# Three PSUM banks for the scores and one for the value products in a global attention loop

## The chip, the cores and the metric

The kernel runs on one NeuronCore of a Trainium2 chip. The metric is the device time of one execution in microseconds (us), as the median of several runs. Four engines compute: PE (TensorE, matrix products; PEld is its weight load), DVE (VectorE), ACT (ScalarE) and POOL (GpSimd). SP (SyncE) issues the transfers. Each engine works through its own queue in order, and the queues are tied together by semaphores alone. PSUM, where PE writes, has eight banks of 512 fp32 columns in each of 128 partitions.

## What is computed

The reference is a transformer block on a batch of 4 sequences of 1024 tokens and 128 channels. A modulated layer norm is followed by global attention with 16 heads of width 8, then by another modulated layer norm and six layers of local attention and a gated feed-forward net. The change is in global attention only:

```
scores = einsum('bhqd,bhkd->bhqk', q, k) / sqrt(8)
attn = softmax(scores, axis=-1)
out = einsum('bhqk,bhkd->bhqd', attn, v)
```

## The kernel before

The function `global_attention` covers 4 batches times 16 heads as `NG` = 16 groups of `GH` = 4 heads. Each group has two halves (`qh`) of 512 queries, and each half has 8 steps, one for each block of 128 keys (`kb`); a group so has 16 steps `s`. A half group is 8 steps. Three kinds of work are interleaved, and the order of each engine is written out by hand.

- **Scores.** `score(g, s, c)` is one matmul of 128 keys by 512 queries for head `c` (line 566), into a bank of `p_s`. ACT takes its exponential into `E` (line 706), in fp32. `p_s` has two banks, so score n waits until exponential n-2 is done.
- **Value products.** `weigh(g, s, halves)` multiplies `E` of the step before with the values, for four heads side by side in four column groups (line 583), and accumulates over the 8 steps into one bank of `p_o` for each `qh`. It is cut into two halves of 256 queries, except for the first key block of a half group, which is done in one piece of 512. It waits for all four exponentials of its step. The value rows carry a one, so that the sum of the exponentials comes out as a further column.
- **Maxima for later work.** The softmax needs the row maxima before the exponentials. A *unit* is two matmuls of 128 queries by 512 keys (line 546) into one of two slots of `p_max`, two banks each, and a DVE reduction over its 1024 columns (line 640). Unit k waits until reduction k-2 is done. A half group needs 16 units. They are computed 11 steps and less ahead, two in each step (`units(g, s)`): the first beside scores 0 and 1, the second beside scores 2 and 3. The rows of the operands are laid out so that a unit and the scores beside it lie in different row halves of the array (rows 0 to 49, and rows 64 to 113), and run together as a pair.

Twice in a group, at `s % 8 == 5`, the 16 unit maxima of a half group are turned by a PE transpose (`max_rows`, line 555), split by DVE into two bf16 parts (lines 649 and 651) and written by four SP transfers (line 491) as two further rows of `QA`. The scores of that half group, from step `s % 8 == 0` on, wait for them on `s_md`. The transpose reads what the last reduction wrote, and it lies in the ring of `p_max` slots. In these steps ("late" in the code) both units of the step come after the transpose, so that scores 0 and 1 have no unit beside them, the first unit is issued with scores 2 and 3 of its own row half, and the second alone.

Twice in a group the value products are finished: ACT copies `p_o` to `OE` (line 697) after the exponentials of step `s % 8 == 2`, PE transposes `OE` back into the same bank of `p_o` at the end of step `s % 8 == 3` (line 591, four transposes), and DVE takes the reciprocal and multiplies into `AO` (lines 658 and 661).

PSUM is full: 4 banks for `p_max`, 2 for `p_s`, 2 for `p_o`. The order on PE in an ordinary step is S0 M1a, S1 M1b, W0, S2 M2a, S3 M2b, W1. Here S is a score, M a matmul of a unit, and W half of a value product, which is of the step before.

Of the kernel before, what the change touches and what calls it, by code (L numbers as in the profile page):

```python
# [9 lines left out]
ALU = mybir.AluOpType  # L10
# [3 lines left out]
P = 128  # L14
# [24 lines left out]
NG = B * HG  # L39
# [381 lines left out]
def global_attention(nc, ins, w):  # L421
# [18 lines left out]
    s_mx = m.count("s_mx", 2 * HU + 2)  # L440
    s_mr = m.count("s_mr", 2 * HU + 2)
    s_mb = m.count("s_mb", 2)
# [4 lines left out]
    s_oe = m.count("s_oe", 2)  # L447
    s_ot = m.count("s_ot", 2)
    s_rc = m.count("s_rc", 2)
    s_ao = m.count("s_ao", 2)  # L450

# [21 lines left out]

    def begun_with(g):

        return [(0, 0, i) for i in range(HU)], [(0, 1, i) for i in range(6)]

    def on_sp(sp):
# [7 lines left out]
        def max_rows(g, qh):  # L486
            sp.wait_ge(s_mr.sem, s_mr.at(g, (qh + 1) * (HU + 1)))
# [46 lines left out]
    def on_pe(pe):  # L534
        pe.wait_ge(s_z.sem, 3)

        def max_unit(g, qh, i, parts=(0, 1)):
            k = qh * (HU + 1) + i
            c, qt = unit(i)
            o, cb = place(c)  # L540
            if 0 in parts and g * (2 * HU + 2) + k >= 2:
                pe.wait_ge(s_mr.sem, g * (2 * HU + 2) + k - 1)
            if 0 in parts and i == 0 and qh == 0:
                pe.wait_ge(s_ld[g % 3].sem, s_ld[g % 3].at(g // 3))
            for j in parts:
                mm = pe.matmul(p_max[:, k % 2, j * 512:(j + 1) * 512],  # L546
                               QA[o:o + MROW, g % 3, qh, cb, qt * P:(qt + 1) * P],
                               KA[o:o + MROW, g % 3, cb, j * 512:(j + 1) * 512], start=True, stop=True)
            if 1 in parts:
                mm.then_inc(s_mx.sem, 1)  # L550

        def max_rows(g, qh):
            k = qh * (HU + 1) + HU
            pe.wait_ge(s_mr.sem, s_mr.at(g, k))
            pe.transpose(p_max[0:GH * 4, k % 2, 0:P], negmax[:, qh, :, :].rearrange("p c q -> p (c q)"),
                         ident[:, :]).then_inc(s_mx.sem, 1)

        def score(g, s, c):
            qh, kb = divmod(s, 8)
            i = 4 * s + c  # L560
            if 64 * g + i >= 2:
                pe.wait_ge(s_ex.sem, 64 * g + i - 1)
            if kb == 0 and c == 0:
                pe.wait_ge(s_md.sem, s_md.at(g, 64 * (qh + 1)))
            o, cb = place(c)
            pe.matmul(p_s[:, i % 2, :], KA[o:o + KROWS, g % 3, cb, kb * P:(kb + 1) * P],  # L566
                      QA[o:o + KROWS, g % 3, qh, cb, :], start=True, stop=True).then_inc(s_st.sem, 1)

        def weigh(g, s, halves):
            qh, kb = divmod(s, 8)  # L570
            if kb == 0:
                if 0 not in halves:
                    return
                lo, hi = 0, 512
            else:
                lo, hi = 256 * halves[0], 256 * (halves[-1] + 1)
            pe.wait_ge(s_ex.sem, s_ex.at(g, 4 * s + 4))
            if s == 0:
# [6 lines left out]
            if hi == 512:  # L585
                mm.then_inc(s_pv.sem, 1)

        def result(g, qh):
            pe.wait_ge(s_oe.sem, s_oe.at(g, qh + 1))
# [4 lines left out]
        before, after = begun_with(0)  # L594
        for u in before:
            max_unit(*u)
        max_rows(0, 0)
        for u in after:
            max_unit(*u)
        for g in range(NG):  # L600
            for s in range(16):
                todo = units(g, s)
                late = s % 8 == 5
                w_ = (g, s - 1) if s > 0 else (g - 1, 15) if g > 0 else None
# [4 lines left out]
                if todo and not late:  # L609
                    max_unit(*todo[0], (1,))  # L610
                if w_:
                    weigh(*w_, (0,))
                if s == 5:
                    max_rows(g, 1)
                if s == 13 and g + 1 < NG:
                    max_rows(g + 1, 0)
                score(g, s, 2)
                if todo:
                    max_unit(*todo[0 if late else 1], (0,))
                score(g, s, 3)  # L620
                if todo:
                    max_unit(*todo[0 if late else 1], (1,))
                if w_:
# [7 lines left out]
        weigh(NG - 1, 15, (0, 1))  # L631
        result(NG - 1, 1)

    def on_dve(dve):

        def max_unit(g, qh, i):
            k = qh * (HU + 1) + i
            c, qt = unit(i)
            dve.wait_ge(s_mx.sem, s_mx.at(g, k + 1))
            dve.tensor_reduce(negmax[:, qh, c, qt:qt + 1], p_max[:, k % 2, :], axis=AX.X, op=ALU.max,  # L640
                              negate=True).then_inc(s_mr.sem, 1)

        def max_rows(g, qh):
            k = qh * (HU + 1) + HU
            dve.wait_ge(s_mx.sem, s_mx.at(g, k + 1))
            if g > 0:
# [7 lines left out]
        def result(g, qh):  # L654
            b, hg = divmod(g, HG)
            dve.wait_ge(s_ot.sem, s_ot.at(g, qh + 1))
            o = p_o[:, qh, :].rearrange("p (q c w) -> p q c w", q=4, w=VW)
            dve.reciprocal(rsum[:, qh, :, :], o[:, :, :, DH]).then_inc(s_rc.sem, 1)
# [3 lines left out]
                              in1=rsum[:, qh, :, :].unsqueeze(3).broadcast_to([P, 4, GH, DH]),  # L662
                              op=ALU.mult).then_inc(s_ao.sem, 1)

        before, after = begun_with(0)
        for u in before:
            max_unit(*u)
        max_rows(0, 0)
        for u in after:
            max_unit(*u)  # L670
        for g in range(NG):
            for s in range(16):
                todo = units(g, s)
                late = s % 8 == 5
                if todo and not late:
                    max_unit(*todo[0])
                if s == 5:
                    max_rows(g, 1)
                if s == 13 and g + 1 < NG:
                    max_rows(g + 1, 0)  # L680
                if todo:
                    max_unit(*todo[0 if late else 1])
                if todo and late:
                    max_unit(*todo[1])
                if s == 3 and g > 0:
                    result(g - 1, 1)
                if s == 11:
                    result(g, 0)
        result(NG - 1, 1)

    def on_act(act):

        def result_copy(g, qh):
            act.wait_ge(s_pv.sem, s_pv.at(g, 8 * (qh + 1)))
            if g > 0:
                act.wait_ge(s_ot.sem, s_ot.at(g - 1, qh + 1))
            act.activation(OE[:, qh, :], p_o[:, qh, :], ACT.Copy).then_inc(s_oe.sem, 1)

        for g in range(NG):
            for s in range(16):  # L700
                for c in range(GH):
                    i = 4 * s + c
                    act.wait_ge(s_st.sem, s_st.at(g, i + 1))
                    if c == 0 and 16 * g + s >= 4:
                        act.wait_ge(s_pv.sem, 16 * g + s - 3)
                    act.activation(E[:, s % 4, c, :], p_s[:, i % 2, :], ACT.Exp, scale=DH ** -0.5)\  # L706
# [1054 lines left out]
```

## Time and profile before

| what | us |
|---|---|
| median of 3 runs | 3910.28 |
| lowest and highest run | 3904.84, 3911.35 |
| span of the profiled execution, first to last instruction | 3903.5 |
| first to last exponential of global attention (line 706) in it | 138.6 to 841.3 |

The profile shows one execution. The span is its time from its first instruction to its last; the page gives no time around it, so that the distance to the median of the runs, 6.8 us, stands for what lies around it and for the spread. Global attention is the stretch from about 111 to 845 us. Before it lie the modulation and the projections, behind it the residual and the six layers, some 3050 us that the change does not touch.

### The profile page before, as it was taken

To read this page: it belongs to the slowest core of one execution; us is meant where nothing else is said; L and a number is where in the kernel's file an instruction comes from. 1 tells how busy PE (TensorE), PEld (TensorE's weight loads), DVE (VectorE), ACT (ScalarE), POOL (GpSimd) and SP (SyncE) were. 2 spreads that over 40 slices of the span, in tenths; PEclk is the share of its full clock that TensorE was granted. 3 is DMA by queue.
4 is the path that set the end of the run, shared out by engine and by line. 5 is a ranking of instruction groups with operands and counts; after the bars stand their busy time and mean duration, and the time that the engine had idled before them with its cause. 6 is when DMAs were issued, how large, how long until landed. Compare 5 with 4: busy or idle time off the path is not lost. (4 is left out here: it accounts for less than half of the span.)

```text
span 3903.5 us, 161387 instructions
## 1 busy us (share of the span) xinstructions
PE 3703.2 (95%) x70608; PEld 2688.4 (69%) x70608; DVE 3274.0 (84%) x4767; ACT 2854.2 (73%) x5060; POOL 2384.1 (61%) x1968
## 2 busy tenths in 40 slices
PE   5899999976999999999999999999999999999997
PEld 3222222235888888888888888888888888888885
DVE  7899899956888888888888888888888888888884
ACT  2488888865777777777777777777777777777774
POOL 2000000017777777877778777777777777777784
PEclk7799999998999999999999999999999999999999
DMA  2110000003444344344443344443443443443442
GB/s 89 34 50 26 18 21 18 14 17 107 113 106 116 103 118 119 103 111 111 111 120 108 104 118 111 113 115 104 110 119 108 116 109 103 130 113 103 115 109 56
DMA packets 202559, 360.11 MB, mean 92 GB/s; under 512 B 35518, under 2 KB 74050, under 8 KB 201538
## 3 DMA queue, kind: packets, MB, share of 16 engines
q1 hardware_dynamic: 201794, 348.71, 33.1%
q8 instruction: 627, 10.27, 1.1%
q14 instruction: 138, 1.13, 0.1%
HBM read 236.68 MB, written 111.67 MB: 89 GB/s over the span
## 5 line engine op out<-in xcount | busy, mean ns | idle before, releaser
L1121 POOL TENSOR_TENSOR T<-T 128x1024 f32<-128x1024 f32 x384 | 908.1, 2377 | 27.0 <-DVE T L1600 26.1
L1139 POOL TENSOR_TENSOR T<-T,rn 128x1024 f32<-128x1024 f32 x384 | 731.4, 1905 | 27.1 <-POOL rn L1132 0.4
L706 ACT ACTIVATE E<-p_s 128x512 f32<-128x512 f32 x1024 | 555.8, 596 | 169.4 <-PE p_s L566 164.2
L640 DVE TENSOR_REDUCE negmax<-p_max 128x1 f32<-128x1024 f32 x512 | 605.7, 1221 | 52.1 <-PE p_max L546 38.6
L1211 PE MATMUL PA<-Wqkv,XS 128*128 128x512 f32 x2304 | 633.3, 410 | 10.0 <-DVE XS L1561 8.1
L1211 PEld LDWEIGHTS PA<-Wqkv,XS 128*128 128x128 f32 x2304 | 415.4, 194 | 80.3 <-DVE XS L1561 10.1
L1608 DVE TENSOR_REDUCE ss<-SQ 128x32 f32<-128x2048 f32 x192 | 436.8, 2275 | 0.0
L1239 PE MATMUL PD<-ident,T 128*128 128x128 f32 x3072 | 409.3, 276 | 6.6 <-POOL T L1139 6.4
L1287 PEld LDWEIGHTS PB<-ET,VW 64*64 64x64 f32 x24576 | 377.1, 135 | 53.9 <-DVE T L1600 29.6
L1287 PE MATMUL PB<-ET,VW 64*64 64x32 f32 x24576 | 399.0, 220 | 15.9 <-DVE T L1600 9.6
L1300 PEld LDWEIGHTS PD<-Wo,OT 128*128 128x128 f32 x3072 | 366.2, 192 | 62.1 <-issue 62.1
L1427 ACT ACTIVATE SQ<-PA 128x1024 f32<-128x1024 f32 x192 | 196.9, 1025 | 271.9 <-PE PA L1211 271.9
L1579 DVE TENSOR_REDUCE sm<-Ew 128x16 f32<-128x1024 f32 x192 | 233.6, 1217 | 190.6 <-ACT Ew L1441 190.6
L566 PE MATMUL p_s<-QA,KA 50*128 50x512 bf16 x1024 | 360.6, 387 | 29.4 <-ACT E L706 14.8
L1300 PE MATMUL PD<-Wo,OT 128*128 128x128 f32 x3072 | 378.6, 277 | 5.1 <-ACT OT L1455 3.1
L546 PE MATMUL p_max<-KA,QA 48*128 48x512 bf16 x1024 | 361.5, 397 | 12.9 <-PEq L417 8.8
L1115 POOL TENSOR_TENSOR Ew<-Ew,sm 128x1024 f32<-128x1024 f32 x192 | 365.7, 1905 | 12.3 <-DVE sm L1584 12.3
L1595 DVE TENSOR_TENSOR T<-PA,tab 128x1024 f32<-128x1024 f32 x192 | 234.4, 1221 | 157.9 <-ACT SQ L1427 157.9
L1239 PEld LDWEIGHTS PD<-ident,T 128*128 128x128 f32 x3072 | 337.9, 141 | 26.8 <-ACT qT L1470 6.0
L1211 PE MATMUL PB<-Wqkv,XS 128*128 128x512 f32 x1152 | 337.4, 428 | 0.0
L583 PE MATMUL p_o<-E,VG 128*32 128x512 f32 (+1 forms) x3832 | 321.9, 408 | 0.1
L1261 PE MATMUL PC<-kT,qT 64*32 64x64 f32 x24576 | 294.1, 224 | 22.3 <-issue 22.3
(168 smaller groups left out, 6809.6 us busy)
## 6 DMA issues: line engine op xcount, KB each, us to landing
VW<-v_rows SPq DMA_DIRECT2D x768, 256.0 KB, 4.4
v_rows<-Vs SPq DMA_DIRECT2D x192, 512.0 KB, 6.0
Wraw<-in_Wqkv SPq DMA_DIRECT2D x40, 192.0 KB, 5.1
QA<-parts_q SPq DMA_DIRECT2D x384, 16.0 KB
KA<-parts_k SPq DMA_DIRECT2D x192, 32.0 KB
parts_q<-parts SPq DMA_DIRECT2D x8, 384.0 KB, 2.6
parts_k<-parts SPq DMA_DIRECT2D x8, 384.0 KB, 2.6
Wo<-in_Wo SPq DMA_DIRECT2D x12, 256.0 KB, 4.8
```

The source lines that it names most:

```text
L546: mm = pe.matmul(p_max[:, k % 2, j * 512:(j + 1) * 512], QA[o:o + MROW, g % 3, qh, cb, qt * P:(qt + 1) * P], KA[o:o + MROW, g % 3, cb, j * ...
L566: pe.matmul(p_s[:, i % 2, :], KA[o:o + KROWS, g % 3, cb, kb * P:(kb + 1) * P], QA[o:o + KROWS, g % 3, qh, cb, :], start=True, stop=True).t ...
L640: dve.tensor_reduce(negmax[:, qh, c, qt:qt + 1], p_max[:, k % 2, :], axis=AX.X, op=ALU.max, negate=True).then_inc(s_mr.sem, 1)
L706: act.activation(E[:, s % 4, c, :], p_s[:, i % 2, :], ACT.Exp, scale=DH ** -0.5)\
L1115: pool.tensor_tensor(out=e, in0=e, in1=sm[:, p, 1, :].unsqueeze(2).broadcast_to([P, LH, KW]), op=ALU.mult).then_inc(pn.sem, 1)
L1121: pool.tensor_tensor(out=t_, in0=t_, in1=T2[:, i * HALF:(i + 1) * HALF], op=ALU.add).then_inc(ad.sem, 1)
L1139: pool.tensor_tensor(out=t_, in0=t_, in1=rn[:, p, i * LH:(i + 1) * LH].unsqueeze(2).broadcast_to([P, LH, LD]), op=ALU.mult).then_inc(no.se ...
L1211: mm = pe.matmul(pair[:, half, :], XS[:, b, i, 1:P + 1], Wqkv[:, l % 2, j, lo:lo + 512], start=(k == 0), stop=(k == 2))
L1239: mm = pe.transpose(flat(PD)[:, j * P:(j + 1) * P], T1[:, n % 2, lo:lo + P], ident[:, :])
L1287: mm = pe.matmul(PB[c * LD:(c + 1) * LD, par, i * P + q:i * P + q + WIN], VW[o:o + KW, p, v, j * LD:(j + 1) * LD], ET[o:o + KW, j, q:q + WIN],
L1300: mm = pe.matmul(PD[:, 0, 0:D], OT[:, j, :], Wo[:, l % 2, j, :], start=(j == 0), stop=(j == PAIRS - 1))
L1608: dve.reduce_sum(ss[:, p, :], heads(SQ[:, :]), axis=AX.X).then_inc(ssq.sem, 1)
```

## The change

`p_s` gets a third bank and `p_o` gives one up. From this follow the other edits:

- Score n takes bank n mod 3 and waits for exponential n-3.
- Both halves `qh` accumulate into the one bank of `p_o`. The first value product of a half group waits until ACT has copied the result of the half group before (`s_oe`). The copy moves from behind the exponentials of step 2 (mod 8) to behind those of step 0. The first key block is cut into two halves like the others.
- The transposed result no longer goes back into `p_o` but takes a slot in the ring of the maxima (`turn`, `turns`). `s_ot` and `s_ao` go; `s_mx` and `s_mr` count all turns of the ring.
- The order in steps 3 and 5 (mod 8) changes: the transposes of the result, or of the maxima, come behind the first half W0 of the value product, between the first and the second unit of the step, on PE as on DVE. The late step goes: its first unit stands beside scores 0 and 1 again and its second beside scores 2 and 3.
- In step 1 (mod 8) score 2 and the first matmul of the second unit come ahead of W0.

```diff
-    p_s = m.ps("p_s", [P, 2, 512])
-    p_o = m.ps("p_o", [P, 2, 512])
+    p_s = m.ps("p_s", [P, 3, 512])
+    p_o = m.ps("p_o", [P, 512])
...
+    ROWS, RESULT = HU, HU + 1
+
+    def extra(g, s):
+
+        if s == 5:
+            return [(g, 1, ROWS)]
+        if s == 13 and g + 1 < NG:
+            return [(g + 1, 0, ROWS)]
+        if s == 3 and g > 0:
+            return [(g - 1, 1, RESULT)]
+        if s == 11:
+            return [(g, 0, RESULT)]
+        return []
+
+    before = [(0, 0, i) for i in range(HU)] + [(0, 0, ROWS)] + [(0, 1, i) for i in range(6)]
+    turns = list(before)
+    for g in range(NG):
+        for s in range(16):
+            turns += units(g, s)[:1] + extra(g, s) + units(g, s)[1:]
+    turns.append((NG - 1, 1, RESULT))
+    turn = {item: k for k, item in enumerate(turns)}
...
+        def free(k):
+            if k >= 2:
+                pe.wait_ge(s_mr.sem, s_mr.at(k - 2))
...
         def score(g, s, c):
             qh, kb = divmod(s, 8)
-            i = 4 * s + c
-            if 64 * g + i >= 2:
-                pe.wait_ge(s_ex.sem, 64 * g + i - 1)
+            n = 64 * g + 4 * s + c
+            if n >= 3:
+                pe.wait_ge(s_ex.sem, n - 2)
...
-            if kb == 0 and g > 0:
-                pe.wait_ge(s_ao.sem, s_ao.at(g - 1, qh + 1))
+            if kb == 0 and half == 0 and g + qh > 0:
+                pe.wait_ge(s_oe.sem, s_oe.at(g, qh))
             for c in range(GH):
-                mm = pe.matmul(p_o[c * VW:(c + 1) * VW, qh, lo:hi], VG[:, g % 2, kb, c, :], E[:, s % 4, c, lo:hi],
-                               start=(kb == 0), stop=(kb == 7), skip_group_check=True)
+                mm = pe.matmul(p_o[c * VW:(c + 1) * VW, lo:hi], VG[:, g % 2, kb, c, :], E[:, s % 4, c, lo:hi],
+                               start=(kb == 0 and half == 0), stop=(kb == 7), skip_group_check=True)
...
         def result(g, qh):
+            k = turn[g, qh, RESULT]
+            free(k)
             pe.wait_ge(s_oe.sem, s_oe.at(g, qh + 1))
             for qt in range(4):
-                mm = pe.transpose(p_o[:, qh, qt * P:(qt + 1) * P], OE[:, qh, qt * P:(qt + 1) * P], ident[:, :])
-            mm.then_inc(s_ot.sem, 1)
+                mm = pe.transpose(p_max[:, k % 2, qt * P:(qt + 1) * P], OE[:, qh, qt * P:(qt + 1) * P], ident[:, :])
+            mm.then_inc(s_mx.sem, 1)
...
                 score(g, s, 0)
-                if todo and not late:
-                    max_unit(*todo[0], (0,))
+                if one:
+                    max_unit(one, (0,))
                 score(g, s, 1)
...
+                if s % 8 == 1:
+                    score(g, s, 2)
+                    if two:
+                        max_unit(two, (0,))
+                if done:
+                    weigh(*done, 0)
+                for item in extra(g, s):
+                    turned(item)
+                if s % 8 != 1:
+                    score(g, s, 2)
+                    if two:
+                        max_unit(two, (0,))
                 score(g, s, 3)
-                if todo:
-                    max_unit(*todo[0 if late else 1], (1,))
-                if w_:
-                    weigh(*w_, (1,))
-                if todo and late:
-                    max_unit(*todo[1])
-                if s == 3 and g > 0:
-                    result(g - 1, 1)
-                if s == 11:
-                    result(g, 0)
+                if two:
+                    max_unit(two, (1,))
+                if done:
+                    weigh(*done, 1)
...
-                if s == 2 and g > 0:
+                if s == 0 and g > 0:
                     result_copy(g - 1, 1)
-                if s == 10:
+                if s == 8:
                     result_copy(g, 0)
```

## Rows read from the trace of the kernel before

**Rows 1.** Busy time by stretch: length; PE, PEld, DVE, ACT, POOL; granted clock, DMA share, GB/s.
```profile
230.00:670.00 440.00, 421.49 (x3787) 120.10 (x3788) 398.67 (x402) 357.61 (x664) 11.46 (x13) 1.00 0.09 24
```

**Rows 2.** Line 658, once per half group: 230:670, then all; first, last start.
```profile
L658 DVE RECIPROCAL rsum<-p_o x20: 247/248/248, 239.5 to 657.2; 128x16 f32<-128x16 f32 x20
L658 DVE RECIPROCAL rsum<-p_o x32: 247/248/258, 173.5 to 844.4; 128x16 f32<-128x16 f32 x32
```

**Rows 3.** Waits in 230:670: engine, line, releaser: total us, times, longest.
```profile
PEld p_s L566 <- ACT E L706: 178.2, 400, 1.0
```

**Rows 4.** PE in time order (start, length, instruction, count): scores 0 and 1 of a step.
```profile
533.52 0.39 PE L566 MATMUL p_s<-QA,KA 50*128 50x512 bf16 x1
...
533.95 0.39 PE L566 MATMUL p_s<-QA,KA 50*128 50x512 bf16 x1
```

**Rows 5.** PE in time order: half a step in which no score waits.
```profile
520.65 0.39 PE L566 MATMUL p_s<-QA,KA 50*128 50x512 bf16 x1
...
520.88 0.38 PE L566 MATMUL p_s<-QA,KA 50*128 50x512 bf16 x1
...
521.19 0.64 PE L583 MATMUL p_o<-E,VG 128*32 128x256 f32 x8
521.76 0.39 PE L566 MATMUL p_s<-QA,KA 50*128 50x512 bf16 x1
```

**Rows 6.** Last matmul of a unit, its reduction; two scores, their exponentials.
```profile
519.76 0.39 PE L546 MATMUL p_max<-KA,QA 48*128 48x512 bf16 x1
520.22 1.23 DVE L640 TENSOR_REDUCE negmax<-p_max 128x1 f32<-128x1024 f32 x1
527.62 0.60 PE L566 MATMUL p_s<-QA,KA 50*128 50x512 bf16 x2
528.04 1.08 ACT L706 ACTIVATE E<-p_s 128x512 f32<-128x512 f32 x2 [0.26 <-PE p_s L566]
```

**Rows 7.** PE near the end, no units left: scores that begin two successive steps.
```profile
818.30 0.81 PE L566 MATMUL p_s<-QA,KA 50*128 50x512 bf16 x2
...
820.75 0.81 PE L566 MATMUL p_s<-QA,KA 50*128 50x512 bf16 x2
```

**Rows 8.** PE in time order: transposed result, next score; transposed maxima.
```profile
524.57 0.66 PE L591 MATMUL p_o<-ident,OE 128*128 128x128 f32 x4
525.16 0.39 PE L566 MATMUL p_s<-QA,KA 50*128 50x512 bf16 x1
...
528.72 0.28 PE L555 MATMUL p_max<-ident,negmax 128*16 128x128 f32 x1
```

**Rows 9.** DVE in time order, with the idle time before and its releaser.
```profile
525.28 0.25 DVE L658 RECIPROCAL rsum<-p_o 128x16 f32<-128x16 f32 x1
...
525.84 2.57 DVE L640 TENSOR_REDUCE negmax<-p_max 128x1 f32<-128x1024 f32 x2
529.03 0.28 DVE L649 CAST nmb<-p_max 16x128 bf16<-16x128 f32 x1 [0.62 <-PE p_max L555]
529.35 0.28 DVE L651 TENSOR_TENSOR nmb<-p_max,nmb 16x128 bf16<-16x128 f32 x1
530.00 6.88 DVE L640 TENSOR_REDUCE negmax<-p_max 128x1 f32<-128x1024 f32 x6 [0.38 <-PE p_max L546]
```

**Rows 10.** The last value products (512 wide) and the copy behind them.
```profile
841.91 0.16 PEld L583 LDWEIGHTS p_o<-E,VG 128*32 128x32 f32 x8 [0.63 <-ACT E L706]
843.05 0.60 ACT L697 ACTIVATE OE<-p_o 128x512 f32<-128x512 f32 x1 [1.19 <-PE p_o L583]
```

**Rows 11.** Busy time by stretch; the last two columns are DMA share and GB/s.
```profile
534.00:535.00 1.00, 1.00 (x12) 0.30 (x12) 1.00 (x2) 1.00 (x2) 0.00 (x0) 1.00 0.00 0
```

**Rows 12.** Near the start: a stretch (granted clock 0.50), and PE in it.
```profile
145.70:149.00 3.30, 3.30 (x24) 0.67 (x24) 2.42 (x3) 1.86 (x4) 0.00 (x0) 0.50 0.00 0
146.78 0.60 PE L566 MATMUL p_s<-QA,KA 50*128 50x512 bf16 x1
...
148.76 0.59 PE L566 MATMUL p_s<-QA,KA 50*128 50x512 bf16 x1
```

More of the change, by code:

```diff
@@ L535, in on_pe, with max_unit @@
         pe.wait_ge(s_z.sem, 3)
-        def max_unit(g, qh, i, parts=(0, 1)):
-            k = qh * (HU + 1) + i
+        def free(k):
+            if k >= 2:
+                pe.wait_ge(s_mr.sem, s_mr.at(k - 2))
+        def max_unit(item, parts=(0, 1)):
+            g, qh, i = item
+            k = turn[item]
             c, qt = unit(i)
             o, cb = place(c)
-            if 0 in parts and g * (2 * HU + 2) + k >= 2:
-                pe.wait_ge(s_mr.sem, g * (2 * HU + 2) + k - 1)
+            if 0 in parts:
+                free(k)
             if 0 in parts and i == 0 and qh == 0:
@@ L552, in max_rows @@
         def max_rows(g, qh):
-            k = qh * (HU + 1) + HU
-            pe.wait_ge(s_mr.sem, s_mr.at(g, k))
+            k = turn[g, qh, ROWS]
+            free(k)
+            pe.wait_ge(s_mr.sem, s_mr.at(turn[g, qh, HU - 1]))
             pe.transpose(p_max[0:GH * 4, k % 2, 0:P], negmax[:, qh, :, :].rearrange("p c q -> p (c q)"),
@@ L565, in score, with weigh @@
             o, cb = place(c)
-            pe.matmul(p_s[:, i % 2, :], KA[o:o + KROWS, g % 3, cb, kb * P:(kb + 1) * P],
+            pe.matmul(p_s[:, n % 3, :], KA[o:o + KROWS, g % 3, cb, kb * P:(kb + 1) * P],
                       QA[o:o + KROWS, g % 3, qh, cb, :], start=True, stop=True).then_inc(s_st.sem, 1)
-        def weigh(g, s, halves):
+        def weigh(g, s, half):
             qh, kb = divmod(s, 8)
[L571 to L576, printed above, removed]
+            lo, hi = 256 * half, 256 * (half + 1)
@@ L592, in result, with turned @@
-            mm.then_inc(s_ot.sem, 1)
[L594 to L599, printed above, removed]
+                mm = pe.transpose(p_max[:, k % 2, qt * P:(qt + 1) * P], OE[:, qh, qt * P:(qt + 1) * P], ident[:, :])
+            mm.then_inc(s_mx.sem, 1)
+        def turned(item):
+            g, qh, i = item
+            if i == ROWS:
+                max_rows(g, qh)
+            elif i == RESULT:
+                result(g, qh)
+            else:
+                max_unit(item)
@@ L600, in on_pe @@
+        for item in before:
+            turned(item)
         for g in range(NG):
             for s in range(16):
-                todo = units(g, s)
-                late = s % 8 == 5
-                w_ = (g, s - 1) if s > 0 else (g - 1, 15) if g > 0 else None
+                one, two = units(g, s) or (None, None)
+                done = (g, s - 1) if s > 0 else (g - 1, 15) if g > 0 else None
                 score(g, s, 0)
-                if todo and not late:
-                    max_unit(*todo[0], (0,))
+                if one:
+                    max_unit(one, (0,))
@@ new lines, in on_pe @@
+                if done:
+                    weigh(*done, 0)
+                for item in extra(g, s):
+                    turned(item)
+                if s % 8 != 1:
+                    score(g, s, 2)
+                    if two:
+                        max_unit(two, (0,))
+                score(g, s, 3)
+                if two:
+                    max_unit(two, (1,))
+                if done:
+                    weigh(*done, 1)
+        for half in range(2):
+            weigh(NG - 1, 15, half)
@@ L662, in result, with turned @@
                               in1=rsum[:, qh, :, :].unsqueeze(3).broadcast_to([P, 4, GH, DH]),
[L663 to L670, printed above, removed]
+                              op=ALU.mult).then_inc(s_mr.sem, 1)
+        def turned(item):
+            g, qh, i = item
+            if i == ROWS:
+                max_rows(g, qh)
+            elif i == RESULT:
+                result(g, qh)
+            else:
+                max_unit(item)
+        for item in before:
+            turned(item)
         for g in range(NG):
             for s in range(16):
[L673 to L688, printed above, removed]
+                for item in units(g, s)[:1] + extra(g, s) + units(g, s)[1:]:
+                    turned(item)
         result(NG - 1, 1)
@@ L695, in result_copy @@
             if g > 0:
-                act.wait_ge(s_ot.sem, s_ot.at(g - 1, qh + 1))
-            act.activation(OE[:, qh, :], p_o[:, qh, :], ACT.Copy).then_inc(s_oe.sem, 1)
+                act.wait_ge(s_mx.sem, s_mx.at(turn[g - 1, qh, RESULT]))
+            act.activation(OE[:, qh, :], p_o[:, :], ACT.Copy).then_inc(s_oe.sem, 1)
         for g in range(NG):
```

47 lines of the change are left out of this document (18 added, 29 removed).

## The prediction

> **What bounds the kernel now.** I read the busy time by stretch first. Between 230 and 670 us no engine is full: DVE is busy 398.67 of 440 us (91%), ACT 357.61 (81%), and the clock is granted in full [rows 1]. PE's 96% there is no evidence, since pipelined matmuls look longer than they are. Next comes the period. The reciprocal runs once per half group, and 20 of them span 417.7 us, so that a half group takes 417.7 / 19 = 21.98 us [rows 2]. Third, the waits: the largest of PE is that of a score for an exponential, 178.2 us in 400 pieces [rows 3].
>
> Last, one step in time order. Scores 0 and 1 start 0.43 us apart where one waits [rows 4] and 0.23 us where none does [rows 5]. Score n needs the bank of exponential n-2, and ACT takes 0.49 us from one exponential to the next (1.08 less 0.59) and starts 0.42 us behind its score [rows 6]. A half step without a wait is 0.23 to the second score, 0.31 to the value product and 0.57 to the next score, 1.11 us together [rows 5], and a step 2.22. A step really takes 2.45, also near the end, where no unit and no reduction is left [rows 7]. So it is not DVE that sets the ordinary step, but two score banks: 0.23 us a step.
>
> The rest of 21.98 is 21.98 - 8 x 2.45 = 2.38 us. It lies in the transposed result (0.59 us of PE [rows 8]), the transposed maxima, and the late step, where units and scores don't run as pairs. There DVE stands idle 0.62 us ahead of the maxima and 0.38 behind them [rows 9].
>
> **Part 1, the third bank.** Score n then waits for exponential n-3. In a free half step score 2 comes 1.11 us after score 0 and score 3 at 1.34. The exponential of score 0 starts at 0.42, lasts 0.59, and frees its bank at 1.06 (0.04 for the signal, as between lines 649 and 651: 0.32 less 0.28 [rows 9]). Both are free, and PE alone could do a step in 2.22.
>
> **Part 2, the late step.** Its unpaired matmuls go, two slots of PE of 0.23 for each of two units, some 0.9 us per half group. The transposed maxima hide behind the reduction of the unit ahead of them.
>
> **What is late next: DVE.** Six reductions run back to back in 6.88 us, (6.88 - 1.22) / 5 = 1.13 each [rows 9]. Sixteen take 18.12 us. The reciprocal and product take 0.56 (525.28 to 525.84), the two parts of the maxima 0.32 + 0.28. That is 19.28 us per half group, while PE needs 8 x 2.22 + 0.59 + 0.28 = 18.6. PE runs only 0.04 us a step ahead of DVE, so DVE paces.
>
> **The ring's bubbles.** A reduction starts 0.46 us after its last matmul [rows 6], and the slot is free 1.22 + 0.04 = 1.26 after its own start. Let R be the start of a reduction.
> - Ordinary: unit k starts at R(k-2) + 1.26, its reduction could start at + 0.23 + 0.46, so at 1.95. DVE is free at 2 x 1.13 = 2.26. No bubble, 0.31 spare.
> - Result (step 3): the turn between the units takes a slot. The second unit waits for the first reduction: 1.26 + 0.69 = 1.95 after it. DVE would be free at 1.13 + 0.56 = 1.69. Bubble 0.26. The transposes start one value product behind the first pair, and reach DVE 0.71 later (524.57 to 525.28), at 1.13 after the first reduction's start: just in time.
> - Maxima (step 5): likewise, 1.95 against 1.13 + 0.60 = 1.73. Bubble 0.22.
> - Step 1: W0 stands between the two matmuls of the second unit: 1.26 + 0.31 + 0.57 + 0.46 = 2.60 against 2.26. Bubble 0.34.
>
> So a half group takes 19.28 + 0.82 = 20.1 us, 1.88 less than now. The trace has no result in the ring. Bounds: 19.3, if the bubbles vanish, and 20.8, if scores still wait (second rival).
>
> **Part 3, one bank for value products.** The last half product of a half group (W1 of step 0 of the next) is followed by the copy, and the copy by W0 of step 1. The eight records of a half product end 0.64 us after its start [rows 5]. With a signal (0.04), the copy (0.60) and a signal W0 may start 1.32 us after W1 began. An upper bound is the product of 512 queries, which reached its copy 1.14 us after its start [rows 10]: 1.78. In between PE has 0.57 of W1, then 0.23 + 0.23 for three pairs, and 0.31: 1.34. On PE alone that just covers it. Where the ring holds the second unit back (the bubble of step 1), W0 comes 0.34 us later and there is 0.36 to spare. I take nothing; the upper bound would cost 0.1 a half group. If the cover were gone, each us of delay would cost one per half group, with score 3 and its unit queued behind on PE, and DVE waiting for that unit. The copy also moves ahead of the exponentials of step 1 on ACT, which slip by some 0.3 us; the third bank takes that up. The first key block in two parts takes two half steps like all others: nothing.
>
> **Part 4, the maxima's rows.** SP's four transfers follow line 651, whose start is 529.35, and by 534.0 no DMA moves anything [rows 11]: under 4.65 us. Now line 651 starts 1.13 + 0.32 = 1.45 after the first reduction of step 5, and score 0 of step 8 comes 1.95 + 5 x 1.13 = 7.6 less 0.69, less up to 0.2 of lead, = 6.7 after it. That leaves 5.3 us: covered, by 0.6 at least. SP's head loads are issued at other times, and are not moved past anything.
>
> **The sum.** From the first reciprocal, at 173.5, on, 29 intervals are of the ordinary kind [rows 2]: 29 x 1.88 = 55. Before it lie 11 steps, from the first exponential at 138.6 on. The first of them run at half clock, where a half step takes 1.98 us [rows 12] and an exponential is done in time: nothing. The 8 or so behind them save a half group's worth, 2. In the last group, steps 5 to 15 have no unit and PE paces; those and the step behind save 0.23 each [rows 5, 7], 12 x 0.23 = 2.8, less 0.1 for the last product in two parts. Together 60 us. The span of 3903.5 becomes 3844. The median of the runs lies 6.8 above the span, so 3910.3 - 60 = **3850 us**.
>
> **A rule weighed.** DVE is the busiest engine that can be judged, at 91% [rows 1]. The Trainium skill (Perfetto Trace Analysis, "Identifying the Most-Contended Engine") wants the engine with the highest occupancy optimized first. By that rule two score banks would matter little. The row speaks against it, since a step is as long without DVE's work [rows 7]. By the rule part 1 brings nothing and the time is that of the second rival below, 3875; by the row it is 3850.
>
> **Rivals.**
> - *The bubbles vanish.* The lead of PE is enough, and DVE runs through at 19.3. For it: six back to back reductions. Against: in steps 1, 3 and 5 the slot, not PE, is late. 29 x 0.82 = 24 more, 3826 us. Chance 0.08.
> - *The third bank's gain doesn't arrive.* The value product waits for all four exponentials; in a free step the last of them ends less than 0.1 us before W0 is due, so that a slightly longer chain would hold PE in place of the score. Steps stay at 2.45; the late step's part and the rest remain: 8 x 2.45 + 0.59 + 0.28 + 0.34 = 20.8, saving 1.17 x 29 + 1 = 35, 3875 us. Against: DVE's pace loosens it by 0.04 a step. Chance 0.15.
> - *No gain at all*, since the single bank or the rows of the maxima eat it: 3903 to 3915. Chance 0.03.
> - *Slower: the single bank is a chain.* If the copy came 0.36 + 1.88 = 2.2 us later than worked out, W0 of step 1 would hold PE, then DVE, for longer than all that is saved; each further us costs 31 us. Against: only a copy that starts behind the exponentials of step 1 would be so late (four take some 2.5 us), and the order on ACT excludes that. At 3.2 us later: 3941. Chance 0.03.
> - *Slower: the clock falls.* At 0.50 a half step took 1.98 us [rows 12] against 1.11. If more than 15% of the stretch ran so, the gain would be gone; at 30% some 3945 us. Against: the grant is 1.00 over 440 us though PE waits 400 times for a bank [rows 1, 3], and the change takes waits away. Chance 0.02. The Trainium skill (TensorE: Matmul & The Clock Gate, "A second HAM failure mode: psum-queue depth-cycling") tells of a kernel whose cycling through banks made the grant swing between both levels; this trace, which cycles two rings of banks, doesn't agree.
>
> **How the numbers follow.** Forecast 3850, its own band 3840 to 3862, chance 0.69. The range must hold 0.8: 3834 to 3876 takes in the second rival, but leaves out most of the first. A run of this kernel tells 0.2%, 8 us, from no change; faster has 0.69 + 0.08 + 0.15 = 0.92, same 0.03, slower 0.05.
>
> **What would show it.** Reciprocals 20.1 us apart. Waits of line 566 for ACT nearly gone, those of line 546 for DVE up. DVE near 96% busy, with a gap of 0.2 to 0.35 us in steps 1, 3 and 5. No idle time of PE ahead of W0 in step 1. It would be wrong if ordinary steps stayed at 2.45, if the period were above 20.8, or if the layers behind the stage moved.

## The result and the profile after

The changed kernel takes 3849.6 us (median of 4 runs, 3847.4 to 3853.6) against 3910.8 for the kernel before (median of 4 runs, 3904.8 to 3917.0). The ratio is 0.984, with a 95% interval of 0.982 to 0.985: 1.6% faster. Measured again in later rounds it was 0.984 (0.982 to 0.986).

| what, us | before | after |
|---|---|---|
| median | 3910.8 | 3849.6 |
| span of the profiled execution | 3903.5 | 3851.6 |
| one half group | 21.98 | 20.06 |
| first exponential (138.6, 137.9) to last reciprocal (844.4, 781.6) | 705.8 | 643.7 |

The stage gives back 62 us. The two spans differ by only 52. The remaining 10 lie behind the stage, in layers whose code is the same; other runs of the changed kernel had spans of 3845 to 3848, so I take this for the spread of single executions; the medians are 61 us apart. The profiled run of the changed kernel took 3853.6 us as timed from outside and 3851.6 by its span, so that 2 us lie around a span and not 6.8. The rest of the 6.8 was spread.

Busy time by stretch of the changed kernel, columns as in [rows 1]:

```profile
230.00:670.00 440.00, 430.68 (x4322) 114.31 (x4314) 423.78 (x440) 391.87 (x728) 12.36 (x15) 1.00 0.10 26
```

And its reciprocal, for 230 to 670 us and in all, as in [rows 2]:

```profile
L681 DVE RECIPROCAL rsum<-p_max x22: 246/248/249, 248.1 to 669.6; 128x16 f32<-128x16 f32 x22
L681 DVE RECIPROCAL rsum<-p_max x32: 246/248/258, 167.9 to 781.6; 128x16 f32<-128x16 f32 x32
```

DVE has gone from 398.67 to 423.78 of 440 us, 96%. Most reciprocals are 20.06 apart; in three intervals between 248 and 349 us it is 20.12, so that the 22 here give 421.5 / 21 = 20.07. In each of those three (at 254.5, 294.7 and 334.9 us) ACT has one more copy to make, of a weight for the layers behind (line 728). The order of DVE, to be held against [rows 9]:

```profile
501.94 2.35 DVE L662 TENSOR_REDUCE negmax<-p_max 128x1 f32<-128x1024 f32 x2
504.56 4.62 DVE L662 TENSOR_REDUCE negmax<-p_max 128x1 f32<-128x1024 f32 x4 [0.27 <-PE p_max L567]
509.10 0.25 DVE L681 RECIPROCAL rsum<-p_max 128x16 f32<-128x16 f32 x1
509.38 0.29 DVE L684 TENSOR_TENSOR AO<-p_max,rsum 128x128 f32<-128x128 f32 x1
509.87 4.63 DVE L662 TENSOR_REDUCE negmax<-p_max 128x1 f32<-128x1024 f32 x4 [0.20 <-PE p_max L567]
514.42 0.27 DVE L671 CAST nmb<-p_max 16x128 bf16<-16x128 f32 x1
514.72 0.28 DVE L673 TENSOR_TENSOR nmb<-p_max,nmb 16x128 bf16<-16x128 f32 x1
515.20 9.15 DVE L662 TENSOR_REDUCE negmax<-p_max 128x1 f32<-128x1024 f32 x8 [0.20 <-PE p_max L567]
```

One half group is all in these rows. DVE stands idle three times, 0.27 us in step 1, 0.20 behind the result in step 3, 0.20 behind the maxima in step 5, and the rows show no other idle time. The 0.62 and 0.38 around the maxima [rows 9] are gone. PE in time order, the second half of step 0 and the first of step 1:

```profile
521.19 0.39 PE L588 MATMUL p_s<-QA,KA 50*128 50x512 bf16 x1
...
521.42 0.38 PE L588 MATMUL p_s<-QA,KA 50*128 50x512 bf16 x1
...
521.73 0.64 PE L600 MATMUL p_o<-E,VG 128*32 128x256 f32 x8
522.30 0.39 PE L588 MATMUL p_s<-QA,KA 50*128 50x512 bf16 x1
...
522.75 0.39 PE L588 MATMUL p_s<-QA,KA 50*128 50x512 bf16 x1
523.27 0.39 PE L567 MATMUL p_max<-KA,QA 48*128 48x512 bf16 x1
523.59 0.64 PE L600 MATMUL p_o<-E,VG 128*32 128x256 f32 x8
```

Scores 2 and 3 of step 0 start 0.23 us apart: no score waits. In step 1 (from 522.30) score 2 goes at once, and the unit beside it 0.52 us later, when its slot is free. W0 follows at the usual distance, 0.32, so the copy does not hold it.

One view misleads. The waits of line 588, the score, for ACT have not "nearly gone":

```profile
PEld p_s L588 <- ACT E L720: 136.9, 351, 0.4
PEld p_max L567 <- DVE negmax L662: 27.6, 66, 0.6
```

There are 351 of them, of 0.4 us at most, where [rows 3] had 400, up to 1.0. This is the idle time of the *weight load*. Its loads for a value product take 0.16 us, the product 0.57, and the next score's load comes 0.41 after them whether anything holds it or not; the view puts the gap to the semaphore that the load checks. Of the 178.2 us of [rows 3] most was this too, by an estimate: 0.41 us behind each of some 300 value products make 123. The waits of the unit's load for DVE did go up, as forecast, from 9.8 us in 20 pieces to 27.6 in 66. What told the bank's price was the distance between two score matmuls, 0.43 against 0.23 [rows 4, 5].

### The profile page after: what moved, and what is told of

Read it like the earlier page. It is cut to its first block and busy times, and to the rows that moved or that the text cites. A ratio compares the mean times of both kernels' runs of the same rounds, so it can differ in the third digit from the quotient of the medians.

```text
span 3851.6 us, 161980 instructions
## 1 busy us (share of the span) xinstructions
PE 3659.9 (95%) x70872; PEld 2666.8 (69%) x70872; DVE 3254.8 (85%) x4767; ACT 2855.0 (74%) x5060; POOL 2384.5 (62%) x1968
## 3 DMA queue, kind: packets, MB, share of 16 engines
q14 instruction: 138, 1.13, 0.1%
## 5 line engine op out<-in xcount | busy, mean ns | idle before, releaser
L662 DVE TENSOR_REDUCE negmax<-p_max 128x1 f32<-128x1024 f32 x512 | 589.5, 1218 | 29.3 <-PE p_max L567 29.3
L567 PE MATMUL p_max<-KA,QA 48*128 48x512 bf16 x1024 | 324.2, 394 | 25.6 <-DVE negmax L662 12.4
L600 PE MATMUL p_o<-E,VG 128*32 128x256 f32 x4096 | 327.9, 392 | 0.6 <-ACT E L720 0.4
L588 PE MATMUL p_s<-QA,KA 50*128 50x512 bf16 x1024 | 320.6, 385 | 0.0
```

The costliest lines, as they stand in the source:

```text
L567: mm = pe.matmul(p_max[:, k % 2, j * 512:(j + 1) * 512], QA[o:o + MROW, g % 3, qh, cb, qt * P:(qt + 1) * P], KA[o:o + MROW, g % 3, cb, j * ...
L600: mm = pe.matmul(p_o[c * VW:(c + 1) * VW, lo:hi], VG[:, g % 2, kb, c, :], E[:, s % 4, c, lo:hi], start=(kb == 0 and half == 0), stop=(kb = ...
```

## The experiments

Theory: (a) before, the two score banks set the pace of ordinary steps, not DVE; (b) in the changed kernel DVE sets it, plus a bubble (a gap on DVE that comes back in every half group) at each of three places of the ring of slots; (c) the single bank for value products costs nothing as long as its copy is covered. Rivals: DVE paced both kernels and the gain is the late step's; PE or the exponentials pace both; the bubbles are late transposes. The time of a half group is the distance that nearly all neighbouring reciprocals of a trace have.

**The third bank taken away again.**

```diff
-    p_s = m.ps("p_s", [P, 3, 512])
+    p_s = m.ps("p_s", [P, 2, 512])
...
-            if n >= 3:
-                pe.wait_ge(s_ex.sem, n - 2)
+            if n >= 2:
+                pe.wait_ge(s_ex.sem, n - 1)
```

> The changed kernel with all its new orders, but with two score banks: score n waits for exponential n-2 again. My theory (two score banks hold PE 0.23 us in each ordinary step, and DVE's pace is not what set the kernel before): seven steps of 2.45, and step 1, where score 2 now has to wait for the exponential behind the copy, of some 3.1, with 0.59 + 0.21 for the transposes: 20.8 to 21.0 us per half group against 20.06, so 22 to 27 us slower than the changed kernel, 3872 to 3877. Rival (DVE alone paces and the third bank is idle, all the gain is the late step's): 20.06 and 3850, within 4 us.

Measured: 3896.6 us, ratio to the kernel before 0.997 (0.995 to 0.998); a half group takes 21.49. The third bank is worth 1.43 us a half group in this order, and the rival that gave it nothing falls. My number, 20.8 to 21.0, was too low by 0.5 or more. PE in step 1 (mod 8):

```profile
506.87 0.38 PE L588 MATMUL p_s<-QA,KA 50*128 50x512 bf16 x1
...
507.92 0.39 PE L588 MATMUL p_s<-QA,KA 50*128 50x512 bf16 x1 [0.67 <-ACT E L720]
...
509.70 0.39 PE L588 MATMUL p_s<-QA,KA 50*128 50x512 bf16 x1
```

Score 2 waits for the exponential that now stands behind the copy, as expected; the step takes 3.06. The miss is in steps 3 and 5. I had added the transposes' time on PE (0.59 and 0.21), but the unit behind them waits for its slot, and both steps take 3.08, 0.63 more than an ordinary one. 3.06 + 2 x 3.08 + 5 x 2.45 = 21.5. Step 1 holds 0.61 more than an ordinary step, and 0.24 more than step 1 of the kernel before, which takes 2.82: by the row, score 2 waits 0.67, and in that kernel it doesn't wait there. The new order of step 1 and place of the copy cost this where there are two banks.

**The late step put back.** Three score banks, but steps 3 and 5 in the order of the kernel before; the order of the ring's turns, and of DVE, follows.

```diff
+                late = s % 8 == 5
+                beside = one if late else two
                 score(g, s, 0)
-                if one:
+                if one and not late:
                     max_unit(one, (0,))
...
+                if late and two:
+                    max_unit(two)
+                if not late:
+                    for item in extra(g, s):
+                        turned(item)
```

> The changed kernel with three score banks, but with the order of the kernel before in steps 3 and 5 (mod 8): the result's transposes at the end of the step, the maxima's ahead of both units. My theory: the maxima's turn has nothing to hide behind, so that DVE stands idle some 0.45 us ahead of it and 0.43 behind it in place of 0.20 in all, while the result's bubble stays about 0.25: some 20.7 us per half group against 20.06, 15 to 22 us slower than the changed kernel, 3865 to 3872. Rival (the late step's cost is taken up by the three banks, PE has lead enough): within 4 us of 3850.

Measured: 3875.6 us, 0.991 (0.989 to 0.993); a half group takes 20.95, 0.89 more than in the changed kernel. DVE around the maxima:

```profile
509.04 0.28 DVE L685 CAST nmb<-p_max 16x128 bf16<-16x128 f32 x1 [0.62 <-PE p_max L583]
509.35 0.28 DVE L687 TENSOR_TENSOR nmb<-p_max,nmb 16x128 bf16<-16x128 f32 x1
510.01 10.27 DVE L676 TENSOR_REDUCE negmax<-p_max 128x1 f32<-128x1024 f32 x9 [0.38 <-PE p_max L573]
```

The 0.62 and 0.38 of [rows 9] are back to the digit. I had worked out 0.45 and 0.43; the first is longer because PE has the value product to issue between the last reduction and the transpose. So the order of steps 3 and 5, the late step above all, is worth 0.9 of the 1.92, and what is left for the third bank and the rest is 1.0. The two prices, 1.43 and 0.89, add up to more than 1.92, since each was taken with the rest of the change in place, and with two banks that rest has the wait of 0.67 in step 1. No run shows the third bank without the other edits; its bank comes from `p_o`.

**Half a reduction, in both kernels.** Each maximum is taken over the first 512 keys; the softmax is then shifted by another number. The edit is the same in both:

```diff
-            dve.tensor_reduce(negmax[:, qh, c, qt:qt + 1], p_max[:, k % 2, :], axis=AX.X, op=ALU.max,
+            dve.tensor_reduce(negmax[:, qh, c, qt:qt + 1], p_max[:, k % 2, 0:512], axis=AX.X, op=ALU.max,
```

> The kernel before with each maximum taken over 512 of the 1024 keys. My theory (in the kernel before the two score banks pace the ordinary step): ordinary steps stay at 2.45; only PE's waits for a reduction in the late step can go, 0.41 ahead of the maxima's transpose and 0.49 behind it: 21.98 falls to between 21.1 and 21.98, 0 to 28 us faster than the kernel before, 3882 to 3911. Rival (DVE, the busiest engine, paced it): the half group falls to 19 or less, 85 us or more faster, below 3830.

> The changed kernel with each maximum taken over 512 of the 1024 keys, so that a reduction takes about half the time; the softmax is shifted by another number, which changes rounding alone or lets exponentials grow. My theory (DVE paces the changed kernel): the pace passes to PE, 8 x 2.21 + 0.59 + 0.21 = 18.5, plus 0.2 of waiting for the copy in step 1: 18.7 us per half group against 20.06, some 40 us faster than the changed kernel, 3805 to 3813. Rival (the chain of scores and exponentials, or PE, still paces): 20.06, 3845 to 3853.

Measured on the kernel before: 3888.2 us, 0.995 (0.993 to 0.997); a half group 21.60, 0.38 less. With 0.5 us less work in each of 16 reductions, little moves. The 0.38 does not come from the late step, where I had looked for it (step 5 still takes 3.3), but from steps 1 and 6, which fall from 2.82 to 2.61 and from 2.61 to 2.45. DVE's share falls from 91% to 56% (245.74 of 440), the ordinary step stays at 2.45, and a score still waits in it; here it is score 3:

```profile
510.58 0.39 PE L566 MATMUL p_s<-QA,KA 50*128 50x512 bf16 x1
...
511.03 0.39 PE L566 MATMUL p_s<-QA,KA 50*128 50x512 bf16 x1
```

Measured on the changed kernel: 3807.9 us, 0.974 (0.972 to 0.976); a half group 18.89, 1.17 less. Now DVE waits in each half step, and PE paces at 1.11:

```profile
513.42 0.69 DVE L662 TENSOR_REDUCE negmax<-p_max 128x1 f32<-128x512 f32 x1 [0.41 <-PE p_max L567]
514.53 0.69 DVE L662 TENSOR_REDUCE negmax<-p_max 128x1 f32<-128x512 f32 x1 [0.41 <-PE p_max L567]
```

The same edit is worth 0.38 us in the one and 1.17 in the other. That is (a) and (b) in one pair: the change moved the pace of the ordinary step from the score banks to DVE. At 18.9 it is PE that paces, with 0.2 of waiting for the copy in it.

**Step 1 in the ordinary order.** W0 ahead of score 2.

```diff
-                if s % 8 == 1:
-                    score(g, s, 2)
-                    if two:
-                        max_unit(two, (0,))
                 if done:
                     weigh(*done, 0)
...
-                if s % 8 != 1:
-                    score(g, s, 2)
-                    if two:
-                        max_unit(two, (0,))
+                score(g, s, 2)
+                if two:
+                    max_unit(two, (0,))
```

> The changed kernel, with the order of step 1 (mod 8) as in all other steps: W0 ahead of score 2 and of the second unit. My theory: the bubble of step 1 (0.34 worked out) goes, and a wait of W0 for the copy comes in its place. By the changed kernel's trace the copy ends 1.52 us after W1 began and W0 would be due at 1.11: 0.41 of waiting, of which DVE's lead leaves 0.24. Half group 19.9 to 20.0 against 20.06, some 3 us faster than the changed kernel, 3846. Rival (the order of step 1 is needed to cover the copy on the one bank for value products): half group 20.4 or more, 10 us or more slower.

Measured: 3848.2 us, 0.983 (0.980 to 0.986); a half group 20.02. The trace shows the trade: W0 now waits for the copy, and DVE's gap of step 1 is 0.24 in place of 0.27.

```profile
506.02 4.62 DVE L657 TENSOR_REDUCE negmax<-p_max 128x1 f32<-128x1024 f32 x4 [0.24 <-PE p_max L567]
```

The answer on `p_o` for 230 to 670 us says how long the value products waited for the copy (us, times):

```profile
  ACT OE L706: 9.5, 22
```

That is 0.43 us each time. 0.04 us a half group is about 1 us, which the times can't tell from nothing. The special order of step 1 neither helps nor hurts the changed kernel.

**One turn of the ring for both transposes.** The maxima and the result share a slot in step 5, each in its own bank; step 3 becomes ordinary.

```diff
         if s == 5:
-            return [(g, 1, ROWS)]
-        if s == 13 and g + 1 < NG:
-            return [(g + 1, 0, ROWS)]
-        if s == 3 and g > 0:
-            return [(g - 1, 1, RESULT)]
-        if s == 11:
-            return [(g, 0, RESULT)]
+            return [(g, 1, ROWS)] + ([(g - 1, 1, RESULT)] if g > 0 else [])
+        if s == 13:
+            return ([(g + 1, 0, ROWS)] if g + 1 < NG else []) + [(g, 0, RESULT)]
         return []
...
-            pe.transpose(p_max[0:GH * 4, k % 2, 0:P], negmax[:, qh, :, :].rearrange("p c q -> p (c q)"),
+            mm = pe.transpose(p_max[0:GH * 4, k % 2, 512:512 + P], negmax[:, qh, :, :].rearrange("p c q -> p (c q)"),
```

> The changed kernel with one turn of the ring for both the maxima's and the result's transposes, in step 5 (mod 8), each in a bank of its own of the slot; step 3 becomes ordinary. My theory (a turn between two reductions costs a bubble because the next unit waits for the slot of the reduction ahead, 1.95 us after its start whatever DVE does in between): 1.13 + 0.56 + 0.60 = 2.29 of DVE's work fill 1.95, so that both bubbles, 0.22 and 0.20 in the trace, go: 19.6 to 19.65 us per half group, 12 to 13 us faster than the changed kernel, 3837. Rival (the gaps come from PE's transposes being late, not from the slot): five transposes in a row make the gap longer, 20.1 or more, no gain.

Measured: 3832.4 us, 0.980 (0.977 to 0.982); a half group 19.45. Five transposes now come one behind the other, yet the gaps are gone. The unit behind them starts 1.27 us after the start of the reduction ahead (503.38 less 502.11), as it does behind the one transpose in step 5 of the changed kernel (514.55 less 513.28): it was the slot that was late.

```profile
503.24 0.27 DVE L680 CAST nmb<-p_max 16x128 bf16<-16x128 f32 x1
503.55 0.28 DVE L682 TENSOR_TENSOR nmb<-p_max,nmb 16x128 bf16<-16x128 f32 x1
503.75 0.23 DVE L690 RECIPROCAL rsum<-p_max 128x16 f32<-128x16 f32 x1
504.02 0.29 DVE L693 TENSOR_TENSOR AO<-p_max,rsum 128x128 f32<-128x128 f32 x1
504.23 9.13 DVE L668 TENSOR_REDUCE negmax<-p_max 128x1 f32<-128x1024 f32 x8
513.63 9.14 DVE L668 TENSOR_REDUCE negmax<-p_max 128x1 f32<-128x1024 f32 x8 [0.27 <-PE p_max L572]
```

It gained 0.61 us where 0.43 was expected. In a row, the four small pieces take 0.99 (503.24 to 504.23); I had added 1.16 from distances at which each had waited for its own semaphore.

**Both edits together**, twice, the second time beside the changed kernel on the same chip.

> Both edits together, the joint turn and the ordinary step 1: 19.5 us per half group, 16 us faster than the changed kernel, 3834. If the order of step 1 is needed, it is slower than the joint turn alone.

> The changed kernel as it is, on the same chip and in the same rounds as the two behind it, so that they can be compared with it: 3850, and reciprocals 20.06 us apart.

> The joint turn with the ordinary step 1 once more. Its trace gave 19.22 us per half group, 0.84 less than the changed kernel: 29 x 0.84 = 24 us faster than it, 3826. If its 3827 came from the chip and not from the ring, it is within 8 us of the changed kernel.

Measured: 3827.2 us, 0.978 (0.976 to 0.980), and again 3826.0, 0.978 (0.977 to 0.980), against 3848.8 for the changed kernel beside the second, 0.984 (0.982 to 0.986), with 20.05 us per half group. Both have 19.22. So the joint kernel is 23 us faster than the changed one and 88 faster than the one before. The view shows no gap of DVE any more in all eight steps:

```profile
499.57 0.29 DVE L688 TENSOR_TENSOR AO<-p_max,rsum 128x128 f32<-128x128 f32 x1
499.78 18.31 DVE L663 TENSOR_REDUCE negmax<-p_max 128x1 f32<-128x1024 f32 x16
518.01 0.27 DVE L675 CAST nmb<-p_max 16x128 bf16<-16x128 f32 x1
```

Something is left all the same. The 16 reductions take 18.23 us (499.78 to 518.01), 0.13 more than 16 x 1.131: in step 1 two of them start 1.25 us apart, too little for the view to show.

The ordinary step 1, worth 0.04 alone, is worth 0.23 here. The traces show why. At best a reduction starts 0.46 us behind its last matmul, and what there is above that is PE's lead, which grows by some 0.025 with each unit. The two bubbles at the transposes set it back to nothing, so that it had come to 0.15 us when step 1 came, in the run of the ordinary step 1 alone; with them gone it comes to 0.31. The wait for the copy is about 0.4 in both.

**A piece taken from DVE.** On top of the joint kernel, the first bf16 part of the maxima is cut by ACT.

```diff
-            dve.tensor_copy(nmb[:, qh, 0, :], rows).then_inc(s_mb.sem, 1)
...
+            act.activation(nmb[:, qh, 0, :], p_max[0:GH * 4, k % 2, 512:512 + P], ACT.Copy).then_inc(s_mb.sem, 1)
...
+                    if s == 5 and c == 1:
+                        rows_copy(g, 1)
+                    if s == 13 and c == 1 and g + 1 < NG:
+                        rows_copy(g + 1, 0)
```

> The joint turn with the ordinary step 1, and the first bf16 part of the maxima taken by ACT between two exponentials in place of DVE (line 671 of the changed kernel). Theory: DVE is busy 99% of the time in the kernel without this edit, so each piece taken from it counts: 0.30 less per half group, of which the slot's bound (1.95 us from reduction to reduction) gives back some 0.13: 19.05 us, 5 us faster, 3821. Rival (PE or ACT already as late as DVE): 19.2 or more, no gain or a loss through the piece queued on ACT.

Measured: 3829.0 us, 0.979 (0.977 to 0.981); 19.22 per half group, no gain at all. I had looked for the answer in step 5. The trace has it in step 1:

```profile
501.77 0.29 DVE L685 TENSOR_TENSOR AO<-p_max,rsum 128x128 f32<-128x128 f32 x1
502.07 9.14 DVE L663 TENSOR_REDUCE negmax<-p_max 128x1 f32<-128x1024 f32 x8
511.46 9.14 DVE L663 TENSOR_REDUCE negmax<-p_max 128x1 f32<-128x1024 f32 x8 [0.24 <-PE p_max L572]
```

A gap of 0.24 is open in step 1. It comes just behind the copy (509.47), for which W0 waits 0.43 us, about as long as in the joint kernel. What has changed is PE's lead: with 0.3 us less of DVE's work at the joint turn, the slot behind it is late again (the reductions around it start 1.90 apart, and not 2.12), the lead begins at nothing there, and it has come to 0.14 in step 1 in place of 0.31. What step 5 gains, 0.22, step 1 gives back. By this trace the copy on the single bank is the next thing that is late; no run of its own tests that.

**The copy two exponentials later.** The price of the single bank, in the changed kernel.

```diff
-                if s == 0 and g > 0:
-                    result_copy(g - 1, 1)
-                if s == 8:
-                    result_copy(g, 0)
+                    if s == 1 and c == 1 and g > 0:
+                        result_copy(g - 1, 1)
+                    if s == 9 and c == 1:
+                        result_copy(g, 0)
```

> The changed kernel with the copy of the value products two exponentials later on ACT, behind those of scores 0 and 1 of step 1. It tests the price of the single bank. My theory: the copy then ends some 0.77 us after the time at which W0 of step 1 starts now, PE waits, and each of these us costs one per half group: 20.8, 22 us slower than the changed kernel, 3872. Rival (PE's lead over DVE hides it): within 5 us of the changed kernel.

Measured: a half group 20.91, 0.85 more; W0 of step 1 waits, as expected:

```profile
540.72 0.64 PE L600 MATMUL p_o<-E,VG 128*32 128x256 f32 x8 [0.79 <-ACT OE L711]
```

But the time was 3889.7 us, 0.994 (0.991 to 0.996), 18 more than 3872. Of its five runs one took 3875.1, close to what was expected, with a mean granted clock of 0.980 over the whole run; the other four took 3888.2 to 3892.3, at 0.974 and 0.975. The trace of one of the four shows where: in the last group, which has no units from step 5 on. Busy time by stretch, then PE:

```profile
784.00:788.00 4.00, 4.00 (x40) 0.91 (x32) 0.00 (x0) 3.95 (x8) 0.00 (x0) 1.00 0.01 1
788.00:792.00 4.00, 2.70 (x22) 0.64 (x20) 0.00 (x0) 3.25 (x7) 0.00 (x0) 0.87 0.02 4
792.00:796.00 4.00, 4.00 (x24) 0.70 (x21) 0.00 (x0) 1.68 (x3) 0.00 (x0) 0.50 0.00 0
```

```profile
790.94 1.08 PE L600 MATMUL p_o<-E,VG 128*32 128x256 f32 x8 [1.30 <-ACT OE L711]
```

PE waited 1.30 us for the copy, and the granted clock fell from 1.00 to 0.50, the lower of its two levels, and stayed there to the end of the stage. The last two half groups took 24.3 and 21.4 us, against 19.0 and 12.8 in the changed kernel: 13.8 us. With 29 x 0.85 = 24.7 for the others, that makes 3888 of 3849.6.

## Why the prediction was right, point by point

- **The bound of before.** Right for the ordinary step. Half a reduction moved that kernel by 0.38 us a half group, so DVE did not set it; the third bank and the late step did. The reading of the other 2.38 us was incomplete. Step 1 had 0.37 of it, as it held the product in one piece of 512, during which no score is issued, while the next score still waited for its bank:

```profile
362.56 0.39 PE L566 MATMUL p_s<-QA,KA 50*128 50x512 bf16 x1
...
363.31 1.06 PE L583 MATMUL p_o<-E,VG 128*32 128x512 f32 x8
...
365.38 0.39 PE L566 MATMUL p_s<-QA,KA 50*128 50x512 bf16 x1 [0.47 <-ACT E L706]
```

From the first score of step 1 to that of step 2 it is 2.82, and not 2.45. The forecast did not suffer, since it built the new half group from DVE's work and not from what the old one would lose. What cutting the product in two is worth by itself, no run shows.

- **The half group.** 20.1 was forecast, 20.06 came. 16 reductions at 1.13, the small pieces, and the three bubbles stand in the trace where they were put: 0.27, 0.20 and 0.20 idle against 0.34, 0.26 and 0.22. The start distances give 0.36 in step 1 (523.13 to 524.62, less 1.13). An idle time in brackets is shorter than the bubble, since a reduction is shown 1.21 to 1.23 us long, and they follow each other at 1.13.
- **The late step.** Forecast as 0.9 of PE's time; with three banks, putting it back costs 0.89. The agreement is partly chance. What it costs is not PE's time (PE has some to spare) but DVE's two idle pieces, 0.62 + 0.38, where the changed kernel has 0.20. By start distances, the reductions around the maxima are 2.82 us apart with the late step and 1.92 without it.
- **The single bank.** Nothing, as forecast; the copy ends at 523.2 and W0 starts at 523.6. The copy itself began 0.86 us behind W1 and not 0.68, since ACT was still at its fourth exponential, a term that my sum left out. The cover (0.36 worked out) was still enough. Its price, one us for one us, was about right: with the copy later, W0 waited 0.79 and a half group took 0.85 more.
- **The sum.** 29 half groups: 55.6 saved against 55. From the first exponential to the first reciprocal 5.0 against 2, after the 30th 1.5 against 2.7. Some 1.2 us have only changed sides, because the result's transposes now come earlier in their step: the reciprocal starts 1.9 us behind the step's first score, and before it was 3.5. The rest of the first term, 1.8, was mis-sized: the granted clock rose earlier, with 1.00 from 146 to 149 us where [rows 12] have 0.50. That is in part the luck of this execution. In the second profile of the changed kernel the mean grant from 146 to 149 us is 0.73, and the same stretch saves 3.8 and not 5.0. The total is 62 for the stage, 61 by the medians, against 60.
- **The layers behind** did not move beyond the spread.
- **A wrong sign to look for.** "Waits of line 566 for ACT nearly gone" did not come true, as told above, and the 178.2 us in 400 pieces were no evidence for the bank, nor for the clock being safe where PE "waits 400 times for a bank". The sentence on the distance of two scores was.
- **The rivals.** The bubbles did not vanish by PE's lead; a slot is late whatever PE has in hand. They do vanish when the turn between two reductions holds 0.99 us of DVE's work. The gain of the third bank did arrive. The clock did not fall here; it did in the variant with the late copy. The two figures of the clock's rival don't fit together: with 1.98 against 1.11 in each of 464 half steps, 15% would cost 61 us and 30% 121, which gives 3971 and not 3945.
- **The rule of the busiest engine.** It would have misled here, and the measurement decides. DVE was the busiest that can be judged, at 91%, and nearly halving its reductions brought 0.5% of the kernel's time. After the change, at 96%, the same edit brought 1.1%.

## What to carry to other kernels

Work out the half step from start distances in a place where nothing waits, and in one where something does; the difference, times the count, is what the engine could gain, here 8 x 0.23 = 1.84 us of PE's time in a half group. The busy shares pointed elsewhere, and the waits of the weight load had the wrong size. Then ask which engine is late next: DVE left only 1.0 to 1.4 of the 1.84 to the third bank. In a ring of two slots the next product waits for the reduction *before* last, so a short piece of other work between two reductions costs a fixed gap: give such a piece enough company to fill it, here by letting two share a turn. And once an engine has hardly a gap left, take nothing more from it before looking at which covered wait is next; what was taken from DVE in step 5 came back in full in step 1, by the trace in the wait for the copy.

## What the hardware showed that was not expected

A single wait cost more than its length here. In the variant with the late copy PE idled 1.30 us in the last group, at a step that has no units to fill its time, the granted clock went from 1.00 to 0.50, and stayed there for the remaining 30 us of the stage: 13.8 us for that wait and the half clock behind it. One trace shows this; that it was so in four of the five runs is concluded from their times and mean clocks. Waits at the same place, 0.79 to 0.90 us long, passed without a fall in the 30 half groups ahead. Whether it was the length of the wait or the thinner work around it that made the difference, no run tells. The Trainium skill (TensorE: Matmul & The Clock Gate, "A second HAM failure mode: psum-queue depth-cycling") tells of a kernel that cycles through banks, where the short idle times of PE between groups of matmuls made the clock swing between both levels again and again. This run agrees only in that idle time for a bank went before a fall: it was one long wait and one fall, no swing. The kernels before and after, with 1.00 from 150 us to the end of the stage, show neither.
